# Twenty-eight first-choice gathers ahead of the third attention instead of twenty-four, and without clearings between them

## What is computed

```python
logits = x @ gate_w.T + gate_b
probs = jax.nn.softmax(logits, axis=-1)
topk_prob, topk_idx = jax.lax.top_k(probs, K)          # K = 2 of 8 experts
for c in range(K):
    ...
    buf_idx = jnp.where(keep, idx * CAP + pos, n_slots)
    ...
    hmid = jax.nn.relu(jnp.einsum('ecd,edf->ecf', xb, W1) + b1[:, None, :])
    yb = jnp.einsum('ecf,efd->ecd', hmid, W2) + b2[:, None, :]
    ytok = yb.reshape(n_slots, Dm)[jnp.clip(buf_idx, 0, n_slots - 1)]
    y = y + ytok * (prb * keep.astype(prb.dtype))[:, None]
...
x = x + y
x = x + _L2_xattn_ref(_layernorm(x, axis=-1), ctx_1024, mask, ...)
x = x + _L2_ffn_ref(_layernorm(x, axis=-1), L2_ffn_weight, L2_ffn_bias)
```

## Time and profile before

| | |
|---|---|
| median of 3 runs | 1215.56 us (1211.11 to 1216.37) |
| the profiled execution | 1217.59 us |
| its span, first to last instruction | 1215.8 us |
| mean granted TensorE clock, of full speed | 0.937 |
| busy share: TensorE, VectorE, ScalarE, GpSimd | 87%, 71%, 67%, 67% |

### The profile page before, as it was taken

One profiled execution on the slowest core, in us unless ns is written; L12 is line 12 of the kernel. 1 busy time (PEld: TensorE's weight loads), 2 busy tenths in 40 slices (PEclk: granted clock), 3 DMA queues, 4 the chain that ended last, 5 costly groups with the idle time before them and its releaser, 6 DMA issues.

```text
span 1215.8 us, 32094 instructions
## 1 busy us (share of the span) xinstructions
PE 1063.4 (87%) x12044; PEld 880.7 (72%) x12044; DVE 865.2 (71%) x2068; ACT 813.9 (67%) x1691; POOL 809.4 (67%) x899
## 2 busy tenths in 40 slices
PE   7999895999997877787799989988779999997895
PEld 5777674999994555556588777766666777776895
DVE  7988982452227899998165588899968999986442
ACT  3777564877768988872322278877547899974573
POOL 6877687682414888678746877884246777746665
PEclk9999997999998999896899999999899999987898
DMA  6146003465316333301375300000120000001451
GB/s 216 54 132 206 9 28 102 141 206 178 105 53 185 103 86 93 97 21 51 121 212 162 95 15 17 18 28 19 51 63 28 27 20 28 19 2 53 139 154 36
DMA packets 101048, 102.59 MB, mean 84 GB/s; under 512 B 14348, under 2 KB 79120, under 8 KB 100896
## 3 DMA queue, kind: packets, MB, share of 16 engines
q1 hardware_dynamic: 90176, 78.15, 21.3%
q0 software_dynamic: 10720, 22.39, 6.2%
HBM read 57.79 MB, written 43.16 MB: 83 GB/s over the span
## 4 chain that ended last, share of the span: by engine, by line
PE 22%; DVE 13%; POOL 9%; issue 5%; ACT 3%; DMA 1%; POOLq 0%; DVEq 0%; ACTq 0%
POOL F_xbuf L3038 3%; DVE uni L2169 2%; PE bS L1019 2%; PE bP L1028 2%; DVE mx L2173 2%; PE bS L1272 2%; PE b L1039 2%; PE bP L1210 2%; POOL uni L2882 1%; POOL gb L3078 1%; POOL uni L3072 1%; DVE mx L2360 1%; PE bP L1287 1%; PE bS L868 1%; PE b L1272 1%
## 5 line engine op out<-in xcount | busy, mean ns | idle before, releaser
L2882 POOL TENSOR_TENSOR uni<-uni,mx 128x1024 f32<-128x1024 f32 x96 | 182.8, 1904 | 93.9 <-DVE mx L2173 60.3
L3038 POOL DMA_INDIRECT F_xbuf<-rows,idxS x128 | 132.6, 1036 | 56.4 <-issue 25.7
L2822 POOL DMA_INDIRECT gb<-F_ybuf,idxG x104 | 109.2, 1050 | 58.9 <-PE b L771 23.7
L893 PEld LDWEIGHTS b<-Vall,uni 128*64 128x64 f32 x3072 | 103.2, 142 | 39.2 <-ACT uni L1404 21.3
L893 PE MATMUL b<-Vall,uni 128*64 128x18 f32 x3072 | 109.0, 214 | 22.9 <-ACT uni L1404 14.8
L1398 ACT ACTIVATE uni<-uni 128x1024 f32<-128x1024 f32 x96 | 101.4, 1056 | 38.8 <-POOL uni L2882 38.1
L868 PE MATMUL bS<-uni,Qx 64*64 64x256 f32 x1536 | 112.3, 410 | 16.5 <-ACT uni L1361 11.8
L879 PE MATMUL bP<-k_ident,uni 128*128 128x128 f32 x768 | 109.3, 288 | 10.0 <-ACT uni L1398 9.8
L1404 ACT ACTIVATE uni<-bP 128x512 f32<-128x512 f32 x192 | 104.6, 596 | 12.2 <-PE bP L879 10.5
L879 PEld LDWEIGHTS bP<-k_ident,uni 128*128 128x128 f32 x768 | 90.5, 148 | 19.1 <-ACT uni L1398 17.5
L868 PEld LDWEIGHTS bS<-uni,Qx 64*64 64x64 f32 x1536 | 51.9, 139 | 59.0 <-issue 25.2
(11 more groups left out here) (373 smaller groups left out, 2993.0 us busy)
## 6 DMA issues: line engine op xcount, KB each, us to landing
F_xbuf<-zero SPq DMA_DIRECT2D x9, 514.0 KB, 5.1
uni<-F_xbuf SPq DMA_DIRECT2D x9, 514.0 KB, 5.2
uni<-F_xbuf SPq DMA_DIRECT2D x18, 256.0 KB, 3.5
F_ybuf<-uni SPq DMA_DIRECT2D x18, 256.0 KB, 2.5
uni<-ctx_dram SPq DMA_DIRECT2D x32, 128.0 KB
A_keys<-Qx SPq DMA_DIRECT2D x16, 256.0 KB, 2.1
uni<-A_keys SPq DMA_DIRECT2D x16, 256.0 KB
uni<-A_keys SPq DMA_DIRECT2D x32, 128.0 KB
```

Of the source, the lines that this page charges most:

```text
L893: ins = T.matmul(b7[64 * b:64 * b + 64, 144 * i + 18 * c:144 * i + 18 * c + 18], pPT[t % 2][:, 128 * c + 64 * b:128 * c + 64 * b + 64], pV ...
L2822: G.indirect_dma_start(gb[n], None, rows_, bass.IndirectOffsetOnAxis(ap=idxG[:, t, c:c + 1], axis=0)).then_inc(*gathered[n].up)
L2882: g.raises(G.tensor_tensor(s3, s3, mx3[t % 3][:, :].unsqueeze(2).to_broadcast([128, 16, 64]), ALU.subtract), b_sb, L, t)
L3038: G.indirect_dma_start(SP[L][0], bass.IndirectOffsetOnAxis(ap=idxS[:, t, c:c + 1], axis=0), rows3[:, t, :] if L == "F3" else XA[:, t, :], ...
```

## The change

`EARLY` goes from 24 to 28, so the first choices of tiles 24 to 27 are gathered and multiplied at the end of the second experts and no longer in the third attention. The clearings between the gathers of L3078 go. Since 28 isn't a multiple of 8, three formulas that count landings per buffer are written for any number.

```diff
-EARLY = 24
+EARLY = 28
...
-        gathered = [sig(f"gathered{i}", 16, F0=8, F1=3 + EARLY // 8 + (8 if i % 4 >= 2 else (NT - EARLY) // 4),
+        gathered = [sig(f"gathered{i}", 16, F0=8, F1=3 + len(range(i, EARLY, 8)) + (8 if i % 4 >= 2 else len(range(EARLY // 2 + i // 4, NP, 2))),
...
-            return 3 + EARLY // 8 + (v // 2 if c else (v - EARLY // 2) // 2)
+            return 3 + len(range(4 * (v % 2) + 2 * c, EARLY, 8)) + (v // 2 if c else (v - EARLY // 2) // 2)
...
                 if L == "F1":
-                    g.wait_ge(f_c0, L, EARLY - 8 + n)
+                    g.wait_ge(f_c0, L, range(n, EARLY, 8)[-1])
...
                                      bass.IndirectOffsetOnAxis(ap=idxG[:, t, 0:1], axis=0)).then_inc(*gathered[t % 8].up)
-                if t % 4 != 3:
-                    pool_pause(g)
```

## The result

The changed kernel takes 1222.5 us as the median of 20 runs (1216.31 to 1226.26), the kernel before, run in turn with it on the same chip, 1213.38 us (20 runs). The ratio is 1.0057, with a 95% interval of 1.0036 to 1.0079: slower by some 7 us. (The quotient of the two medians is 1.0075; every comparison here goes by the ratio that is given with its interval.) A later comparison of the same pair gave 1.0032 (1.0008 to 1.0057), some 4 us. The forecast was +0.9 us, 1216.5 us, with a range up to 1221 us.

The account below looks back on a forecast made before the run. No engine bounds the kernel everywhere; GpSimd's gathers are on the chain at the end of the second experts. A start +3.0 us later less 2.1 us returned gives +0.9 us, 1216.5 us, range 1211 to 1221 us.

Parts of the forecast that it names:

- the clock at the start: Third attention's start: TensorE's longer wait for tile 1 could hold the clock at 1.2 GHz; 0 to 1 us, taken as 0.
- Where GpSimd leaves: End of second experts: clearings removed, four gathers added and a new wait start the third attention 3.0 us later.
- The stretch: End of second experts: gathers meeting VectorE's multiply-adds take longer, 3.75 us in all, between 2.8 and 5.4 us.
- part 3: Third attention's start: second choices of tiles 0 and 1 wait for buffers shared with first choices 26 and 27; +0.4 us.
- VectorE's last bias addition: End of second experts: L2640 comes 1.6 us late behind first choice 22's multiply-add, but this is hidden.
- rival (c): End of second experts: a closed ring of buffers, multiply-adds and TensorE slips; up to +6.3 us, 1221.9 us; chance 0.10.
- Part 4: Around the third attention's start: L2640 1.6 us late but hidden, and a clock loss of 0 to 1 us taken as 0.
- The return: Third attention, tiles 24 to 27: one gather and one multiply-add fewer each give back 2.1 us.
- part 5: Third attention, 779 to 805 us: VectorE's saving counts, not GpSimd's 5.0 us; -2.1 us, bounds 0 and -5.0 us.
- rival (b): Third attention: GpSimd is the bound in tiles 17 to 24, so 5.0 us come back whole; 1213.6 us; chance 0.13.
- Rival (a): End of second experts: a gather that starts first keeps its 0.95 us and VectorE waits; 1213.5 us; chance 0.10.
- the rule on ports: VectorE and GpSimd share a port pair; whichever starts first holds it all instruction long, so gathers beginning first wouldn't be stretched.

Follow-up runs that it names:

- the change again: The changed kernel run once more for a second trace, against the kernel before: ratio 1.0046 on the first chip, 1.0032 on the third.
- the kernel of 28 with the clearings ahead: The change with 18 clearings run ahead of GpSimd's wait on the stored rows, against the kernel before on the second chip: ratio 1.0033.

## Why the prediction was wrong

The direction was right, the size wasn't: +0.9 us were forecast, and the traces show +4.7 us. The measured 1222.5 us lie 1.5 us past the end of the range. Two terms of the sum make most of the difference, the clock at the start, put at 0, and what follows tile 24, left out of it without a reason.

**Where GpSimd leaves: right.** The forecast was +3.0 us up to tile 1, measured +3.06 us (28.59 to 31.65 us) and +3.11 us for the first transpose. Two terms in it were off and cancelled. The stretch was put at 3.75 us; the stretched gathers took 1.34, 1.39, 2.37 and 1.85 us, 3.15 us over their 0.95 us each. The new wait of part 3 was put at +0.4 us and cost 1.16 us (the plain sequence from 682.57 us gives 683.82 us for the first remaining gather, and it started at 684.98 us). It came one gather sooner than forecast, on first choice 26. The prediction's own terms had it there: first choice 26 would start at 684.0 us, and with 2.43, 0.35 and 0.3 us the first remaining gather would go at 687.1 us and not at 686.5 us. And GpSimd resumed 0.77 us behind the end of that multiply-add (684.21 us) and not 0.3 us; the traces of the change again and of 28 gathers with clearings show 0.77 and 0.78 us too. It isn't VectorE that makes this longer: behind the store, in the kernel of 24 without clearings, the same gather took 0.82 us to start. What the step overlooked: in the kernel before, GpSimd's leave lay only 0.6 to 0.8 us above what the last store allows, so that taking the clearings out alone gives 0.8 us and not 2.4 us. Behind the four added gathers they count in full (31.73 to 34.67 us for the 15 that then stand on the path), and the four gathers with three more clearings cost 6.1 us (28.59 to 34.67 us).

**VectorE's last bias addition: right.** 1.6 us late were forecast and 1.46 us measured (23.03 to 24.49 us behind the mark). Nothing on the path hung on it, and the slower rival (c), which needed it over 2.3 us late, didn't happen.

**The clock at the start: the first failed step.** Part 4 took 0 from a range of 0 to 1 us, "since the fillers move too". They move 1.5 us and the rows 3.1 us, so the gap between them doubled, from 1.51 to 3.17 us; the rows said so at the time. It cost 1.1 us, just past the end of that range. In the traces without stops the mean clock over 18 us around the start falls with the wait ahead of the transpose: 1.00 with 0.76 us (24 gathers without clearings), 0.91 with 1.51 us (before), 0.81 with 3.17 us (the change). With 28 gathers and clearings the wait is 2.18 us, and there a part of the low clock fell on the fillers, which took 7.70 us in place of 6.07 us.

**The return: a little too large.** Forecast -2.1 us, measured -1.52 us between tiles 17 and 24 and -0.22 us ahead of them. It is well shown: from tile 17 to tile 24 the two kernels of 24 gathers in the table take 39.2 us (39.19 and 39.17 us), and all those of 28 take 37.7 us (37.66 to 37.68 us); on the two other chips it is 39.6 to 39.7 us against 37.9 us. The rule of part 5 held, VectorE's saving counts and not GpSimd's 5.0 us, so rival (b) fell. The two groups of four gave 1.56 and 0.52 us as forecast; part of it went into waits on VectorE, as the subtraction of 791.76 us, which waits 1.39 us, where its forerunner had no idle time ahead.

**What the sum didn't hold: the second failed step.** I ended the sum at tile 24 and let the rest of the program follow at an equal distance. It didn't: +1.5 us to tile 31, where the clock fell sooner and stayed low 6.8 us longer, and +0.8 us up to the output, whose cause stays open. From tile 31 to the last scatter the six traces of the table take between 349.6 and 352.2 us, so 0.8 us is within what variants differ by there. Nor are the +1.5 us a fixed price of the change: on the first chip it doesn't pay them. With the 1.1 us and the 0.4 us of return that is all of the distance from +0.9 to +4.7 us. The range, up to 1221 us, was made from the mechanisms' bounds alone and had no room for this.

**Rival (a) and the rule on ports.** Rival (a) fell: the change has four stretched gathers, the longest of 2.37 us, begun 0.16 us ahead of five multiply-adds (665.24 and 665.40 us). In the kernel of 24 without clearings it is 2.08 us (675.77 us, with four multiply-adds from 675.90 us that took 1.13 us as ever). But it isn't so for every gather that meets multiply-adds: the one of 659.80 us, begun 0.43 us ahead of five, took its 0.94 us, and the multiply-adds took 1.39 us both times. The fourteen traces draw the line sharply. 62 gathers of the first choices took over 1.2 us. Each had begun at most 0.36 us ahead of the run of multiply-adds, or while it was under way, and each ended 0.81 to 0.83 us behind the end of that run. The eighteen begun 0.39 us or more ahead of two to five multiply-adds took 0.94 to 0.95 us. So a stretched gather lasts until some 0.8 us behind the end of the run, and five multiply-adds in place of four make it longer by 0.26 us. The Trainium skill (SBUF — State Buffer, "SBUF: two separate sides") lets whichever starts first keep the port pair for its whole instruction; it says so of VectorE instructions with two inputs in SBUF too, against GpSimd instructions that read SBUF. Here the gathers of 665.24 and 675.77 us had started 0.16 and 0.13 us sooner and weren't spared, so the rule doesn't fit them.

## What to carry to other kernels

Before an instruction is taken off an engine's path, look at what its next wait would find: here the twelve clearings were worth 2.4 us on paper and 0.8 us in fact, because GpSimd would then have to wait for a store. A moved step has two prices, its own, and that of the clock in each gap it widens. Here 26 filler products left a gap of 3.17 us and 1.1 us of loss by the clock, and 38 kept the clock up but ended 1.0 us late: where a gap of TensorE is filled with products, the filler has to grow with the gap, and no further. And where a kernel crosses stretches in which the clock is about to fall, allow some microseconds on either side of any sum of a change that shifts it, also when the work there stays the same.

## What the hardware showed unexpectedly

The same instructions with the same busy time ahead of them got a granted clock of 1.00 in one kernel and 0.56 in another (the rows from 809.68 us against those from 812.48 us). It repeats where there are no stops: the two traces of the change in the table show the same mean of 0.80 over the same 26 us, and agree to 0.1 us in time. On the first chip, which has stops, the same program has 0.93 over these 26 us and is 1.5 us shorter from tile 24 to tile 31.

Chips differ in more than speed. On two of the three chips of the experiments the kernel before takes 4 to 5% longer (1269 and 1277 us against 1217 us), and the traces there have stops of TensorE of 1 to 6 us that the profile puts down to no wait: five in the kernel before, together 10.3 us, seven in the change, 13.3 us, nine in the kernel of 28 with the clearings ahead, 25.0 us. On the third chip, and in the two first traces, there is none. The longest, 6.4 us, stands at the fillers, where the second experts end; it lies between the last expert matmuls and the bias addition that waits for them. What causes the stops no run shows.
